# Choosing a spline cell by four conditional copies in PSUM instead of a one-hot product and a sum

## The reference

```python
xn = layernorm(x) * ln_gamma + ln_beta                  # x: 8192 rows of 1024
tile_idx = best tile of the best cluster, by signs      # one of 64 tiles for each row
x_slice = xn[row, 16 * tile_idx + (0..15)]              # 16 numbers of each row
mn, mx = min and max of x_slice over all rows that chose the same tile
u = clip((x_slice - mn) / (mx - mn + 1e-08), 0.0, 1.0 - 1e-06)
gi = clip(int(u * 16), 0, 15)                           # the cell, one of 16
b = spline_bases[tile_idx, j, gi]
s = spline_slopes[tile_idx, j, gi]
delta = (b + s * (u * 16 - gi)) * output_scale[tile_idx]
out = x with delta added in those 16 columns
result = layernorm(x + out)                             # so 2 x everywhere, 2 x + delta in 16 columns
```

## Time and profile before

| | before |
|---|---|
| median of 3 runs | 1353.73 us (1349.59 to 1354.64) |
| the profiled execution | 1354.35 us |
| its span (first to last instruction) | 1352.6 us, so 1.75 us lie around it |
| busy: PE, DVE, ACT, POOL | 86%, 81%, 72%, 62% |
| start of the second part (SP's first own load) | 1150.55 us |
| granted TensorE clock in the second part | 0.50 of 2.4 GHz |
| last POOL instruction starts | 1344.81 us |

### The profile page before, as it was taken

How to read it: one execution, slowest core, us unless ns; L and a number is a source line. 1 busy time by engine, 2 the same in 40 slices (tenths; PEclk the granted TensorE clock), 3 DMA queues, 4 the chain that set the end, 5 groups by cost and what they waited for, 6 DMA issues and landing times. The chain is left out here.

```text
span 1352.6 us, 31939 instructions
## 1 busy us (share of the span) xinstructions
PE 1162.5 (86%) x9410; PEld 737.6 (55%) x9410; DVE 1095.3 (81%) x2426; ACT 972.7 (72%) x1873; POOL 845.0 (62%) x1703
## 2 busy tenths in 40 slices
PE   5799999999999999999999999999999641768600
PEld 4556666666666666666666666666666321412200
DVE  4888988889998899999999999999987545499920
ACT  5568888888888888788888888888887431427870
POOL 3125666767676767676767677676776544123776
PEclk9899999999999999999999999999999775555555
DMA  4013332222322222222222222233331115729995
GB/s 133 32 52 115 116 113 101 98 98 106 117 104 101 100 98 98 98 98 98 98 98 98 98 98 98 99 115 115 115 110 69 68 62 195 289 84 343 405 411 223
DMA packets 63827, 174.94 MB, mean 129 GB/s; under 512 B 11419, under 2 KB 22819, under 8 KB 63782
## 3 DMA queue, kind: packets, MB, share of 16 engines
q1 hardware_dynamic: 57638, 172.27, 34.0%
q0 software_dynamic: 6144, 2.11, 1.1%
HBM read 68.93 MB, written 101.20 MB: 126 GB/s over the span
## 5 line engine op out<-in xcount | busy, mean ns | idle before, releaser
L1001 DVE SCALAR_TENSOR_TENSOR acc<-xT_all,cw_sb,acc 128x256 f32<-128x256 f32 x768 | 354.1, 520 | 6.9 <-ACT acc L708 6.8
L734 ACT ACTIVATE sg<-TX,bet,gam 128x256 f16<-128x256 f32 x256 | 130.2, 559 | 54.7 <-PE TX L431 39.9
L451 PE MATMUL PR<-xT_all,w_sb 128*128 128x256 f32 x512 | 138.8, 395 | 2.1 <-ACT xT_all L672 2.1
L1333 POOL TENSOR_TENSOR AT<-AT,Wm 128x128 f32<-128x128 f32 x224 | 113.7, 508 | 42.5 <-DVE AT L1027 26.8
L463 PE MATMUL WK<-w_sb,tS 128*128 128x512 f32 x256 | 138.3, 622 | 0.0
L708 ACT ACTIVATE acc<-xT_all,cb_sb,cw_sb 128x256 f32<-128x256 f32 x256 | 133.1, 595 | 4.6 <-DVE xT_all L987 2.8
L533 PE MATMUL PR<-shT,w_mg_sb 128*64 128x128 f32 x2048 | 127.8, 278 | 6.4 <-ACT shT L717 6.4
L505 PE MATMUL OB<-th_all,AT 128*128 128x512 f32 x256 | 124.7, 610 | 9.5 <-POOL AT L1333 8.0
L533 PE MATMUL PR<-shT,w_rk_sb 128*64 128x128 f32 x2048 | 125.9, 276 | 0.0
L533 PEld LDWEIGHTS PR<-shT,w_rk_sb 128*64 128x64 f32 x2048 | 110.5, 137 | 26.3 <-issue 26.3
L533 PEld LDWEIGHTS PR<-shT,w_mg_sb 128*64 128x64 f32 x2048 | 112.3, 138 | 18.8 <-issue 12.5
(11 more groups left out here) (214 smaller groups left out, 2662.5 us busy)
## 6 DMA issues: line engine op xcount, KB each, us to landing
xin_all<-in_x SPq DMA_DIRECT2D x32, 1024.0 KB
y_ring<-y_all SPq DMA_DIRECT2D x32, 1024.0 KB, 4.1
y_scratch<-y_all SPq DMA_DIRECT2D x32, 1024.0 KB, 6.1
own<-y_scratch SPq DMA_DIRECT2D x8, 2048.0 KB, 23.9
out<-own SPq DMA_DIRECT2D x8, 2048.0 KB, 17.3
xT_all<-y_scratch SPq DMA_DIRECT2D x3, 2048.0 KB
out<-xT_all SPq DMA_DIRECT2D x3, 2048.0 KB
RX<-RE SPq DMA_DIRECT2D x128, 32.2 KB
```

The lines of the kernel that those rows point to most:

```text
L451: i = pe.matmul(PR[:, 0:T], w0_sb[:, blk, :], xT[b][:, blk, HIST:HIST + T], start=(blk == 0), stop=(blk == NB - 1))
L734: nc.scalar.activation(sg[:, blk, :], TX[:, (blk % 2) * T:(blk % 2 + 1) * T], ACT.Sign, scale=gam[:, blk:blk + 1], bias=bet[:, blk:blk + 1 ...
L1001: v.scalar_tensor_tensor(acc[:, blk, :], xT[b][:, blk, i:i + T], cw_sb[:, blk, i:i + 1], acc[:, blk, :], ALU.mult, ALU.add).then_inc(e_con ...
L1333: q.tensor_tensor(late, late, Wm[:, :, l, :].rearrange("p c (n h) -> p c n h", h=h), ALU.add)\
```

## The change

It does six things.

1. **The cell by copies.** The table is stored with base and slope side by side (column = 32 j + 2 cell + table). The cell is kept as a byte and taken apart into four bits. For each pair `COPY_PREDICATED` moves the upper half of each column's 32 numbers onto the lower half where bit 3 is set (512 elements, in place in PSUM), then a quarter by bit 2 (256), an eighth by bit 1 (128), then a plain copy of two numbers to `bsv` (64) and a conditional copy by bit 0 over it (64). Two pairs are worked alternately, with a wait on the operation of the same pair before. `onehot`, `summed`, `ohg` and `pr` go. Z gets a fourth buffer, over the space of `OT` and `QB`.
2. **Tables on 128 rows.** The first two bfloat16 parts stand one above the other (rows 0 to 63 and 64 to 127), with `ohT` doubled likewise. A fetch is then one matmul over 128 rows of weights and one over 64, instead of three over 64. `turned` makes twice as many transposes, alternately into the lower and the upper half of `OT`. The input tables are loaded twice, by three DMAs more.
3. **Batches** of 4, 8, 12, 12, 12, 12 and 4. `cells` for 4, 8 and 52 blocks. TensorE makes `tables` 0 and 1 before `turned(1)`, only `tables(2)` between, and the rest after `ranges` of all.
4. **Corrections on VectorE.** The 16 corrected numbers come from two VectorE operations for each batch, after the next batch, behind a wait for POOL's coefficients; ScalarE's line 1658 goes.
5. **A fifth own slot**, so that five loads start with the second part and seven follow stores.
6. **The extremes** of 16 blocks go before the second state update of step 33, of 24 before the second key of step 34 (behind its state update), of 16 behind `normed` of step 35.

```diff
-    PRE, OWN = 3, 4
+    PRE, OWN = 3, 5
...
                     if live(g, 4):
                         normed(1, *of(4))
+                        if isinstance(g, int) and g - 4 == NG - 1:
+                            extremes(40, 56)
...
                     if live(g, 2):
                         log_scale(*of(2))
+                        if isinstance(g, int) and g - 2 == NG - 1:
+                            extremes(0, 16)
                     if live(g, 3):
                         decay(1, *of(3))
+                        if isinstance(g, int) and g - 3 == NG - 1:
+                            extremes(16, 40)
...
-                    if isinstance(g, int) and g == NG + 1:
-                        extremes(0, 28)
...
-            BATCHES = (4, 4, 8, 12, 12, 12, 8, 4)
+            BATCHES = (4, 8, 12, 12, 12, 12, 4)
...
                     for j in range(8):
-                        i = pe.transpose(OT[:, j, :], oh[:, :, f * 8 + j], ident_bf[:])
+                        for rows in (slice(0, NT), slice(NT, P)):
+                            i = pe.transpose(OT[rows, j, :], oh[:, :, f * 8 + j], ident_bf[:])
...
-                        for k in range(3):
-                            i = pe.matmul(QB[:, n * 2:(n + 1) * 2], ohT[:, n, :], t3s[:, k, :], start=(k == 0), stop=(k == 2))
+                        pe.matmul(QB[:, n * 2:(n + 1) * 2], ohT[:, n, :], t3s01[:], start=True, stop=False)
+                        i = pe.matmul(QB[:, n * 2:(n + 1) * 2], ohT[0:NT, n, :], t3s2[:], start=False, stop=True)
...
+                        pe.matmul(Z[s % 4][:, cols], ohT[:, 2 * s + j, :], t2s01[:], start=True, stop=False)
+                        i = pe.matmul(Z[s % 4][:, cols], ohT[0:NT, 2 * s + j, :], t2s2[:], start=False, stop=True)
...
+                    for s0 in range(lo // 2, hi // 2, 2):
+                        grids = [Z[(s0 + h) % 4][:].rearrange("p (a g) -> p a g", g=2 * GRID) for h in range(2)]
...
+                        for i in (3, 2, 1):
+                            w = 2 ** (i + 1)
+                            for h in range(2):
+                                if i == 3:
+                                    dve.wait_ge(p_z, s0 + h + 1)
+                                else:
+                                    after(h)
+                                then(h, v.copy_predicated(grids[h][:, :, 0:w], chosen_bit(i, h, w), grids[h][:, :, w:2 * w]))
...
+                        for h in range(2):
+                            after(h)
+                            then(h, v.tensor_copy(to[h], grids[h][:, :, 0:2]))
+                        for h in range(2):
+                            after(h)
+                            v.copy_predicated(to[h], chosen_bit(0, h, 2), grids[h][:, :, 2:4]).then_inc(p_zf, 1)
...
+                    dve.wait_ge(p_coef, k + 1)
+                    link(v.tensor_tensor(outs[:, at, :], w_o[:, at, :], per_token(rs), ALU.mult))
+                    v.tensor_tensor(outs[:, at, :], outs[:, at, :], per_token(o_off), ALU.add).then_inc(p_out, 1)
...
+                cells(HEAD, AHEAD)
                 batch(1)
+                corrections(0)
+                cells(AHEAD, NC)
                 for k in range(2, len(BATCHES)):
                     batch(k)
+                    corrections(k - 1)
+                corrections(len(BATCHES) - 1)
```

More of the change, by code:

```diff
@@ L10 @@
 F16 = mybir.dt.float16
+U8 = mybir.dt.uint8
 U32 = mybir.dt.uint32
@@ L1252, in step @@
                         spline_tables()
-                    if isinstance(g, int) and g == NG + 1:
-                        extremes(0, 28)
-                    if isinstance(g, int) and g == NG + 2:
-                        extremes(28, 44)
-                    if isinstance(g, int) and g == NG + 3:
-                        extremes(44, 56)
                 pipeline(dve, step, 4)
@@ L1517, in stored, with batch_of @@
                 return 16 if u == U - 1 else 16 * (u // NS + 1)
+            def batch_of(n):
+                return max(k for k in range(len(BATCHES)) if starts[k] <= n)
             def slot_id(u):
@@ L1616, in tables @@
                     pe.wait_ge(p_ohTe, (2 * s + 1) // 8 + 1)
-                    if s >= 3:
-                        pe.wait_ge(p_zf, s - 2)
+                    if s >= 4:
+                        pe.wait_ge(p_zf, s - 3)
                     for j in range(2):
-                        for k in range(3):
-                            i = pe.matmul(Z[s % 3][:, j * HALF:(j + 1) * HALF], ohT[:, 2 * s + j, :], t2s[:, k, :],
-                                          start=(k == 0), stop=(k == 2))
+                        cols = slice(j * HALF, (j + 1) * HALF)
+                        pe.matmul(Z[s % 4][:, cols], ohT[:, 2 * s + j, :], t2s01[:], start=True, stop=False)
+                        i = pe.matmul(Z[s % 4][:, cols], ohT[0:NT, 2 * s + j, :], t2s2[:], start=False, stop=True)
                     i.then_inc(p_z, 1)
@@ L1631, in _ @@
                 ranges(0, HEAD)
-                for f in range(1, 4):
-                    turned(f)
-                    tables(f - 1)
-                for f in range(4, NC // 8):
+                tables(0)
+                tables(1)
+                turned(1)
+                tables(2)
+                for f in range(2, NC // 8):
                     turned(f)
@@ L1656, in _ @@
                             .then_inc(p_row, 1)
-                    for n in range(starts[k], starts[k + 1]):
-                        nc.scalar.activation(outs[:, n, :], w_o[:, n, :], ACT.Identity, scale=rs[:, n:n + 1],
-                                             bias=o_off[:, n:n + 1]).then_inc(p_out, 1)
             @block.vector
@@ L1726, in summed @@
-                def summed(s, k):
-                    dve.wait_ge(p_zf, s + 1)
-                    at = 2 * s - starts[k]
-                    v.tensor_reduce(bsv[k % 2][:, at:at + 2, :, :].rearrange("p n k j -> p (n k j)"),
-                                    pr[s % 2][:].rearrange("p n (c g) -> p (n c) g", g=GRID), AX_X, ALU.add).then_inc(p_bb, 1)
+                    link(v.tensor_tensor(c, g, t, ALU.subtract))
+                    v.tensor_tensor(x, x, c, ALU.subtract)
+                    for i in range(4):
+                        b = v.tensor_scalar(bits[i][:, lo:hi, :], c, 2 ** i, None, ALU.bitwise_and)
@@ new lines, in cells, with chosen, then, after @@
+                    link(b)
+                def chosen(lo, hi, k):
+                    ready = [0, 0]
+                    def then(h, ins):
+                        count[0] += 1
+                        ins.then_inc(p_v, 1)
+                        ready[h] = count[0]
+                    def after(h):
+                        dve.wait_ge(p_v, ready[h])
+                    for s0 in range(lo // 2, hi // 2, 2):
+                        grids = [Z[(s0 + h) % 4][:].rearrange("p (a g) -> p a g", g=2 * GRID) for h in range(2)]
+                        cols = [slice(2 * (s0 + h), 2 * (s0 + h) + 2) for h in range(2)]
+                        def chosen_bit(i, h, w):
+                            return bits[i][:, cols[h], :].rearrange("p n j -> p (n j)").unsqueeze(2).to_broadcast([P, 2 * DS, w])
+                        for i in (3, 2, 1):
[6 more added lines that the diff above has]
+                                then(h, v.copy_predicated(grids[h][:, :, 0:w], chosen_bit(i, h, w), grids[h][:, :, w:2 * w]))
+                        to = [bsv[k % 2][:, c.start - lo:c.stop - lo, :, :].rearrange("p n j k -> p (n j) k") for c in cols]
+                        for h in range(2):
+                            after(h)
+                            then(h, v.tensor_copy(to[h], grids[h][:, :, 0:2]))
+                        for h in range(2):
+                            after(h)
+                            v.copy_predicated(to[h], chosen_bit(0, h, 2), grids[h][:, :, 2:4]).then_inc(p_zf, 1)
@@ new lines, in corrections, with per_token @@
+                def corrections(k):
+                    at = slice(starts[k], starts[k + 1])
+                    n = BATCHES[k]
+                    def per_token(a):
+                        return a[:, at].unsqueeze(2).to_broadcast([P, n, DS])
+                    dve.wait_ge(p_coef, k + 1)
+                    link(v.tensor_tensor(outs[:, at, :], w_o[:, at, :], per_token(rs), ALU.mult))
+                    v.tensor_tensor(outs[:, at, :], outs[:, at, :], per_token(o_off), ALU.add).then_inc(p_out, 1)
```

144 lines of the change are left out of this document (65 added, 79 removed).

## The result

The changed kernel takes **1339.29 us** (median of 4 runs, 1338.52 to 1340.58) against 1353.57 for the kernel before (1349.59 to 1354.64) on the same chip: a ratio of 0.990, 95% interval 0.988 to 0.992. The profiled execution took 1339.66 us, with a span of 1337.9. The predicted 1339 is met, but by two misses that cancel: the second part starts 4.2 us sooner than forecast and is 4.6 us longer. The rows that the prediction named show them.

The account below looks back on a forecast made before the run. It took the second part as bound first by VectorE, with DMA nearly idle, then by back-to-back transfers. Start at 1140.0 plus 197.5 length plus 1.75 around gave 1339.25; median forecast 1339 us, range 1326 to 1352.

Parts of the forecast that it names:

- The drain: Moved extremes ahead of the second part: `yn` of group 31 10.7 us earlier, second part starting at 1140.0 instead of 1150.55.
- Transposes: TensorE, way to the first gapless store: a round of 16 in two halves takes 2.35 us, between 2.26 and 3.35.
- Table products: TensorE, alternating 128 and 64 rows: 0.55 us per table matmul, 2.2 per pair for four, before 2.56 for six.
- The ranges: TensorE's 120 small products at 0.085 us each, 10.2 us, ending 37.4 after the second part starts, before 28.8.
- The copies: VectorE: five operations take 1.45 us per pair, 2.9 per group of two, before 2.93 per pair; COPY_PREDICATED priced as a product.
- the rivals at twice and three times a product's price: VectorE's conditional copies cost more: at twice, 1352 us, chance 0.14; at three times, 1368 us, chance 0.07.
- Batches 1 and 2: VectorE in the second part: batch 1 at 49.5 us, batch 2 at 73.5, unit 3 ready to store at 83.5.
- The transfers: DMA behind unit 3's store: 19 transfers at 5.36 us, 101.8, last landing 185.3 after the second part starts, before 187.5.
- The end: POOL waits for the last store, then only its four scatters follow: second part 197.5 us long, before 202.05.
- The sum: Whole kernel: 1140.0 + 197.5 = 1337.5, with 1.75 around it 1339.25, 15.1 less than the profiled 1354.35.
- alternation is free: Rival on TensorE's 128/64-row turns: ranges end 7 us earlier, unit 3 ready at about 75, 1330 us; chance 0.17.

## Why the prediction came out right, point by point

- *The drain: right in its mechanism, 1.7 us too small, and 2.4 more by chance.* Against `nl`, `yn` of group 30 is 10.8 us earlier (9.6 forecast), AT 8.4 (6.7), `yn` of group 31 11.7 (10.7), the second part 12.3 (10.6). POOL's statistics of group 30 took 3.7 us in place of 7.6, and I had taken off 3.7 of these (1085.0 to 1081.3): each step was right within 1.7. It isn't every power that lasts long beside the extremes: the same operation for group 31 took 0.72 us in the kernel before too (at 1113.71). The gather to the last extremes, which was to stay as it was, took 9.7 us in place of 10.3 (1120.25 to 1129.92; 1134.33 to 1144.63). With the 2.45 us lead at `nl`, which the runs give to the execution, the second part starts at 1135.84 and not at 1140.0.
- *Transposes: right.* 2.35 us per round forecast, 1152.71 - 1150.36 = 2.35 measured.
- *Table products: right, and the reason too.* 0.54 apart (0.55); the run with both products of a pair in rows shows that the change of the row count is what costs 0.115.
- *The ranges: mis-sized.* 0.117 each and not 0.085: 14.0 us in place of 10.2. I had both numbers in hand, 0.027 in a row and 0.12 per change, whose sum is near 0.15, and set a value below it, since a short product's time is mostly its passage (it lasts 0.16 to 0.18 us by the rows). The sum is too high and my value too low. They ended 40.5 us after the start of the part, 37.4 forecast.
- *The copies: right.* A group of two pairs takes 2.78 us (2.9). By their own durations, 2 x (0.689 + 0.421 + 0.287 + 0.214 + 0.218), it would be 3.66. The Trainium skill, "VectorE: DVE Perf Modes", section "The DRAIN you can't avoid", has each operation wait for an empty pipe; as durations in a trace go, that is 3.66, and the starts say 2.78. The same section goes on that an operation that isn't held starts earlier, which the prediction left out. This trace agrees with that: ten operations start within 2.78 us. So the rivals at twice and three times a product's price fall. What the conditional copies are worth by themselves no run shows. An estimate: two pairs took 2 x 2.93 us before (from the earlier trace rows) and take 2.78 now, which is 3.1 us less per group and 15 us over the five groups ahead of unit 3. Against that stand the ranges, which end 11.7 us later after the start of the part than before (40.5 for 28.8), and the larger batches.
- *Batches 1 and 2:* sums at 52.4 and 75.2 (49.5 and 73.5), the store of unit 3 at 84.5 (83.5). The cells took 10.5 (11.3), which gave back a little of what the ranges took. My way from the sums to the store adds up to 9.8 us (5.2 and 4.6) and stood at 10.0; it took 9.3.
- *The transfers: right by the yardstick that I used.* I had read the end of the transfers before from the DMA share of a window: 0.63 of 5 us, so 1338. Read so, they end at 1322.8 in the changed kernel (0.57 of the window from 1320, at a full share of 1.02), 187.0 after the start of the part where I put 185.3. Of these 1.7 us, 1.0 is the later store of unit 3, and the rest is 19 transfers at 5.39 and not 5.36.
- *The end: the step that failed, 2.9 us too short.* I let POOL go on with the last unit 0.3 us after that point. But the last store lands at 1325.5 (issued at 1300.51, 25.0 to land), 2.7 us later, and only then does POOL's wait end. The kernel before shows a lag of this size: the first of its last four scatters starts 3 us behind 1338.

```profile
1341.02 0.96 POOL L1581 DMA_INDIRECT out<-outs,gidx  x1 [0.30 <-issue]
```

  The prediction dropped it: 14.6 us from 1338 to the end of the span there, 12.2 here, as if POOL had only been behind its work. (When the last store lands there, its trace doesn't say.) Counted from the landing the end takes 12.4 us in the changed kernel; from the point of the windows 15.1, where 12.2 stood. POOL had no slack either: it was through with the unit before at 1325.46, just as the last store landed.
- *The sum.* 4.2 too late at the start of the second part, 1.7 and 2.9 too short in it. Of the 4.5 that the second part was to gain, 2.2 were in the transfers and 2.3 at the end. By the same windows the transfers gave 0.5 (187.0 for 187.5): before, they ran without a gap from the store of unit 2 at 69.6 (22 of them), now from that of unit 3 at 84.5 (19), 14.9 later against three transfers fewer, 16. The end took 0.5 more (15.1 for 14.6). That the copies, the stacked tables and the fifth slot are worth nothing together is a matter of where batch 2 ends, and taking the fifth slot alone away costs 5. That the total came out at 1339 is luck: the drain was undersized by 1.7, the execution was 2.4 ahead, and the second part was 4.6 too short.

The rival "alternation is free" (1330) was wrong in its reason: the alternation isn't free. The run without alternation in the ranges shows what it would have given: 1328.

## What to carry to other kernels

When the end of a stage is set by transfers in series, find the first store behind which they run without a gap: in six kernels here, the changed one and five variants of it with the same 19 transfers behind the store of unit 3, the span ended 116 to 118 us after that store, whatever VectorE did behind it. In the traces each microsecond ahead of it counted in full. Take one yardstick for the end of a transfer, and the landing where another engine waits for it. Compare kernels by stretches between fixed points of the trace, since the stretch ahead of the edit moved by up to 5 us between executions, as much as many an edit is worth. And count the changes of shape in a loop of tiny products: there the change costs three times the product.

## What the runs showed of the hardware

- A product of 128 rows and one of 64 in turn cost 0.089 us more each for 2 columns (0.117 and 0.028 apart) and 0.115 for 512 (0.54 against 0.425 in the earlier trace rows), at a granted clock of 0.50, the lower level of 1.2 GHz. The Trainium skill, "TensorEngine Tiling (Array Packing)", "Key Properties", has a change of tiling mode drain the engine; these runs give the price for a change of the row count alone.
- A conditional copy of 512 elements from PSUM to PSUM within one bank, with a mask of bytes, lasts 0.689 us (0.421 for 256, 0.287 for 128); doubled, it adds 3.54 - 2.35 = 1.19 us for two more, 0.60 each: the start-to-start price of a product of the same size in the earlier trace rows.
- The small scattered writes, 0.47 MB beside 39.85 from 1220 to 1325, take 6 us out of 105 us of large transfers. The rate is 365 GB/s at 1310 to 1315, where it is 421 without them, but 420 with them at 1295 to 1300. The last scatter is 6.9 us on its way (6.6 is the median), which nothing hides.
- The last large store lands 2.7 us behind the point where the DMA share of the windows says that the transfers are over (1325.5 and 1322.8), 0.9 us in the kernel without scatters (1320.9; the share is 0.99 from 1315 to 1320 and 0.02 behind it).
- Ten small POOL operations took 7.6 and 7.4 us with VectorE's extremes of 28 blocks beside them, and 3.7 us with VectorE idle beside all but the first 0.5 of them.
